# Local attention on one core: how the probabilities are transposed and the side values summed

## The chip, the cores and the metric

The kernel runs on one core of one Trainium2 chip. The metric is the device time of one execution in microseconds (us), the median of several runs.

The core has TensorE (PE in the rows; its weight loads are PEld), VectorE (DVE), ScalarE (ACT), GpSimd (POOL) and the sync engine (SP), each with an instruction queue of its own, worked off in order. They are tied together by semaphores: an instruction adds one when it is done, and another engine's queue stands at a wait until the count is there.

## The reference

Input x is 8 x 2048 x 512. A state-space convolution of it gives x2. On x2, two attentions are computed and added: a light one over all tokens, in windows, and a heavy one over 512 queries and 1024 keys that a routing picks. The change is in the light one:

```python
xn = layernorm(x); q, k, v = split(xn @ w_qkv, 3)        # 8 heads of 64
q, k, v -> windows of 64 tokens
kk, vv = around(k), around(v)      # each window sees the window before, itself, the window after: 192 keys
sim = (q * 64**-0.5) @ kk.T        # a missing neighbour (ends of the sequence) is masked
o = softmax(sim) @ vv
light = o @ w_out
```

All of it is fp32 in value: the big products are made of three fp32r products of high and low parts, the attention's own matmuls and transposes are fp32.

## The kernel before

The phases follow each other: preparation, convolution, light attention (from 570 to 2855 us of the profile), routing lists, heavy attention. Only `light_phase` is touched.

**The pipeline.** The light phase handles tiles of 128 tokens, 128 tiles in all (16 for each of 8 sequences). It is written as a software pipeline with one step per tile, numbered g (j is g modulo 16). Each engine has a function `body(g, j, live, b)` that issues its part of step g. `live(k)` says whether tile g-k exists. In step g, TensorE does, in this order:

1. `first_unit`: one quarter of a projection (q, k or v for 4 tiles at once), 12 matmuls of 512 columns, into PSUM bank `ps_b`
2. the output projection of tile g-10, into `ps_c`
3. a second unit into `ps_a`
4. `scores` of tile g-7 into `ps_s` (for each head and each of two windows, 192 key columns; `key_runs` splits them where the ring of keys or the order of columns breaks them)
5. `attend` of tile g-9 into `ps_d`: transposed probabilities times values, 8 matmuls for the tile's own 128 keys ("main", `pt_main`) and 8 for the two neighbouring half tiles ("side", `pt_side`, values in `val_side`)
6. `turn_side` and `turn_main` of tile g-8: transposes of the probabilities, side into `ps_c`, main of the even heads into `ps_b`, of the odd heads into `ps_a`
7. a third unit into `ps_d`
8. the transpose of the next tile's normalised x into `ps_c`

The four banks are shared: each is written in a step two or three times, and TensorE waits until an engine has copied it away (semaphores `..._kept`). Which unit is which goes round in four steps (`units(j)`): with r = (j + 1) mod 4 the first, second and third unit are

- r = 1: k2, k3, v0
- r = 2: v1, v2, v3
- r = 3: q0, q1, q2
- r = 0: q3, k0, k1 (of the next group)

**Who empties the banks.** VectorE copies the first unit out of `ps_b` (`u1_kept`) and the third out of `ps_d`, ScalarE the second out of `ps_a` (`u2_kept`). Two of these copies have a special place because they overwrite data that the scores of this step still read. In VectorE's body:

```python
first_query = units(j)[0][:2] == ("q", 0)
if live(4) and not first_query: wait(v, u1_made, g - 3); keep_unit(ps_b, units(j)[0], u1_kept)
...
if live(7):                      # waits s_made, then two reductions, neg_max (L1617)
...
if live(4) and first_query:      wait(v, u1_made, g - 3); keep_unit(ps_b, units(j)[0], u1_kept)
```

and in ScalarE's: `if live(7) and (j + 1) % GT in (0, 3): wait(act, s_made, g - 6)` ahead of `keep_unit(ps_a, units(j)[1], u2_kept)`.

**The softmax chain.** VectorE takes the maximum of the scores, ScalarE the exponentials (`exps`, into `prob`), VectorE the reciprocals, GpSimd multiplies `prob` by them (L1684, `p_normed`); TensorE transposes the result in the next step. After `attend`, ScalarE copies `ps_d` to `at_hi` (L1262), VectorE subtracts to `at_lo` (L1624, `o_kept`), and only then may the third unit write `ps_d`: `wait(pe, o_kept, g - 8); unit(ps_d, units(j)[2], u3_made)`.

SyncE issues the loads and stores in order, among them two DMAs per step that bring the neighbours' half tiles of `val` into `val_side`, a step before `attend` uses them.

## Time and profile before

| | us |
|---|---|
| median of 3 runs | 4286.02 (4284.94 to 4286.93) |
| the profiled execution's own time | 4281.34 |
| its span, first to last instruction | 4279.6 |
| light attention in it | about 570 to 2855 |
| PE busy, share of the span | 93% |
| DVE, ACT, POOL busy, share of the span | 66%, 42%, 20% |

A row of the timeline gives the start in us, the time from the first start to the last end in us, the engine, the line, the operation, output <- inputs, the tiling of the matmul array (rows*columns), the shape and the count (x). Ends of matmuls lie behind their starts by the pipeline's depth, so the cost of a group of matmuls is read from the start of one group to the start of the next. [n <-X] at the end means: the engine was idle for n us before it, and X released it.

### The profile page before, as it was taken

The numbers are of one execution on the slowest core, as the hardware profiler recorded it, in microseconds if no ns is written. First come the engines' busy times: TensorE is split into PE (matmuls) and PEld (weight loads), VectorE is DVE, ScalarE is ACT, GpSimd is POOL, SyncE is SP. The second block draws the span as 40 slices with busy tenths as digits, with TensorE's granted clock in tenths as the row PEclk, the third lists the DMA queues.
The fourth block names the chain that finished last, engine by engine and source line by source line (L and its number), as shares of the span: only waits on it lengthen the run. The fifth ranks groups of instructions, "written<-read, shape, count | busy, mean of one in ns | idle before, by whom it ended". The sixth has DMA issues, their size and how long they took to land. (4 is left out here: it accounts for less than half of the span.)

```text
span 4279.6 us, 96921 instructions
## 1 busy us (share of the span) xinstructions
PE 3973.7 (93%) x39328; PEld 3279.4 (77%) x39328; DVE 2820.8 (66%) x5012; ACT 1786.0 (42%) x4746; POOL 877.2 (20%) x663
## 2 busy tenths in 40 slices
PE   6788869999999999989999999968999999999998
PEld 5677757888888888878888888857677677677776
DVE  9888857776766767665555566674755646646546
ACT  7434324344433434434444433222544534534434
POOL 0222202222222222222222222211111011111011
PEclk9899979999999999999999999988999999999999
DMA  9688752222223222211222111122012022022021
GB/s 318 168 231 233 208 173 74 83 93 85 82 85 95 83 83 88 86 50 61 67 64 61 60 60 60 45 87 60 19 43 58 9 55 51 16 53 51 16 45 14
DMA packets 341371, 360.91 MB, mean 84 GB/s; under 512 B 23104, under 2 KB 237376, under 8 KB 340928
## 3 DMA queue, kind: packets, MB, share of 16 engines
q1 hardware_dynamic: 262592, 287.52, 22.5%
q0 software_dynamic: 12288, 33.56, 3.7%
q10 hardware_dynamic: 66048, 33.56, 2.9%
q8 instruction: 322, 5.28, 0.5%
q14 instruction: 121, 0.99, 0.1%
HBM read 228.21 MB, written 76.02 MB: 71 GB/s over the span
## 5 line engine op out<-in xcount | busy, mean ns | idle before, releaser
L1684 POOL TENSOR_TENSOR l_prob<-l_prob,l_inv 128x768 f32<-128x768 f32 x256 | 389.6, 1543 | 1690.9 <-DVE l_inv L1641 1690.9
L1235 ACT ACTIVATE l_prob<-l_ps_s,l_neg_max 128x192 f32<-128x192 f32 x1024 | 420.7, 443 | 7.5 <-DVE l_neg_max L1617 7.3
L2237 ACT ACTIVATE h_prob<-h_ps_s,h_neg_max 128x1024 f32<-128x1024 f32 x256 | 285.6, 1116 | 253.4 <-DVE h_neg_max L2311 253.4
L1617 DVE TENSOR_REDUCE l_neg_max<-l_ps_s 128x4 f32<-128x768 f32 x256 | 233.1, 952 | 238.5 <-PE l_ps_s L1004 219.4
L2308 DVE TENSOR_REDUCE h_neg_max<-h_ps_s 128x1 f32<-128x1024 f32 x256 | 312.3, 1220 | 99.7 <-PE h_ps_s L2100 91.0
L2365 DVE COPY h_probs_t<-h_ps_t 128x512 f32<-128x512 f32 x256 | 176.4, 689 | 143.1 <-PE h_ps_t L2112 142.9
L2127 PEld LDWEIGHTS h_ps_o<-h_probs_t,ahead_then_values 128*64 128x64 f32 x4096 | 221.6, 137 | 44.1 <-issue 43.0
L2127 PE MATMUL h_ps_o<-h_probs_t,ahead_then_values 128*64 128x128 f32 x4096 | 252.5, 276 | 0.0
L2112 PEld LDWEIGHTS h_ps_t<-ident,h_prob 64*128 64x128 f32 x4096 | 152.2, 140 | 121.7 <-ACT h_prob L2237 61.0
L1235 ACT ACTIVATION_READ_ACCUMULATOR l_prob<-l_ps_s,l_neg_max 128x1 f32 x1024 | 235.8, 230 | 0.0
L1004 PEld LDWEIGHTS l_ps_s<-l_k_t,l_q_t 64*64 64x64 f32 x6144 | 189.1, 133 | 48.1 <-issue 44.8
L2112 PE MATMUL h_ps_t<-ident,h_prob 64*128 64x64 f32 x4096 | 183.7, 230 | 44.7 <-ACT h_probs_t L2266 42.4
L1202 ACT ACTIVATE l_k_t<-l_ps_a,w_bias_k 128x512 f32<-128x512 f32 x64 | 44.0, 688 | 427.1 <-PE l_ps_a L721 184.4
L1004 PE MATMUL l_ps_s<-l_k_t,l_q_t 64*64 64x64 f32 (+2 forms) x6144 | 213.8, 277 | 2.9 <-DVE ahead_then_values L1498 2.9
L1363 DVE CUSTOM_DVE_ANT_0 l_dot_out<-ahead_then_values 128x512 f32<-128x512 f32 x240 | 205.8, 857 | 4.2
L719 PE MATMUL l_ps_c<-w_out_hi,l_at_hi 128*128 128x512 f32 x512 | 203.1, 397 | 5.8 <-DVE l_pt_side L1589 4.3
L2026 POOL TENSOR_TENSOR h_att<-w_null_v,h_null_exp 128x512 f32<-128x512 f32 x32 | 33.1, 1036 | 852.0 <-ACT h_null_exp L2274 852.0
L1608 DVE TENSOR_TENSOR l_res<-l_ps_c,l_xres 128x512 f32<-128x512 f32 x128 | 88.2, 689 | 176.9 <-PE l_ps_c L721 176.8
L720 PE MATMUL l_ps_c<-w_out_lo,l_at_hi 128*128 128x512 f32 x512 | 202.5, 395 | 0.0
L721 PE MATMUL l_ps_c<-w_out_hi,l_at_lo 128*128 128x512 f32 x512 | 201.6, 394 | 0.0
L1262 ACT ACTIVATE l_at_hi<-l_ps_d 128x512 fp32r<-128x512 f32 x128 | 76.4, 597 | 268.8 <-PE l_ps_d L1036 268.8
L1678 POOL TENSOR_TENSOR l_xres<-l_xres,w_row 128x512 f32<-128x512 f32 x128 | 179.1, 1399 | 16.9 <-DVE scores_then_results L1363 11.9
(392 smaller groups left out, 10793.2 us busy)
## 6 DMA issues: line engine op xcount, KB each, us to landing
toep_back<-taps_padded ACTq DMA_DIRECT2D x32, 1024.0 KB, 10.3
x<-xg SPq DMA_DIRECT2D x64, 512.0 KB, 8.7
l_xin<-x SPq DMA_DIRECT2D x128, 256.0 KB, 3.3
l_xres<-x SPq DMA_DIRECT2D x128, 256.0 KB, 3.2
l_val_side<-l_val SPq DMA_DIRECT2D x256, 128.0 KB, 3.1
out_dram<-l_res SPq DMA_DIRECT2D x128, 256.0 KB, 2.0
ahead_then_values<-x SPq DMA_DIRECT2D x126, 256.0 KB, 3.1
xin<-in_L_attn_x_dram SPq DMA_DIRECT2D x32, 768.0 KB, 6.3
```

The costliest lines, as they stand in the source:

```text
L719: nc.tensor.matmul(out, lh, rh, start=first, stop=False)
L720: nc.tensor.matmul(out, lh, rl, start=False, stop=False)
L721: return nc.tensor.matmul(out, ll, rh, start=False, stop=last)
L1004: last = nc.tensor.matmul(ps_s[win * WIN:(win + 1) * WIN, h, pair, col:col + n], q_t[rows, pair, t % GT * P + win * WIN:t % GT * P + (win ...
L1235: last = nc.scalar.activation(prob[t % 2][:, h, pair, :], ps_s[:, h, pair, BOTH], ACT.Exp, bias=neg_max[:, t % 2, h, pair:pair + 1], accum ...
L1363: nc.vector.tensor_tensor_reduce(dot_out[:, :], x_tile, w["rt"][:, r], 1.0, 0.0, ALU.mult, ALU.add, to[r]).then_inc(dot_step, 1)
L1617: nc.vector.tensor_reduce(neg_max[:, t % 2, h, :], ps_s[:, h, :, BOTH], AX_X, ALU.max, negate=True).then_inc(max_made, 1)
L1684: nc.gpsimd.tensor_tensor(mine, mine, spread(inv[:, t % 2, h, :], [1, PAIRS], [0, WIN + P]), ALU.mult).then_inc(p_normed, 1)
L2112: last = nc.tensor.transpose(ps_t[half][:, n, :], prob[i % 2][rows, n * P:(n + 1) * P], ident[rows, rows])
L2127: last = nc.tensor.matmul(ps_o[odd * DH:(odd + 1) * DH, k * P:(k + 1) * P], val[:, n, h * DH:(h + 1) * DH], probs_t[(2 * pair + odd) % 4][ ...
L2237: nc.scalar.activation(prob[i % 2][:, :].rearrange("p (a k) -> p a k", a=2), ps_s[i % 2][:, :, :], ACT.Exp, bias=neg_max[:, qt % 2, h:h + ...
L2308: nc.vector.tensor_reduce(at, ps_s[i % 2][:, :, :].rearrange("p a k -> p (a k)"), AX_X, ALU.max, negate=True).then_inc(max_step, 1)
```

## The change

- Transposes of main probabilities (`turn_main`): 16 of half the rows each (64 queries x 128 keys, with the 64 x 64 corner of the identity), alternately into `ps_b` (first window) and `ps_a` (second window); before, 8 of 128 x 128.
- Transposes of side probabilities (`turn_side`): `prob` is laid out so that the side columns of the two heads of a pair lie next to each other, and 4 transposes of 128 x 128 do what 16 matmuls with half an identity did. The columns of the even and odd head are laid out differently (`MAIN`, `SIDE`), and `key_runs` follows.
- Sums over side values (`attend_side`): 16 matmuls of 64 keys x 64 outputs x 64 queries, each on the rows that its head uses; before, 8 with 128 keys and 128 queries, half of them zeros. `pt_side` has half the size; the zeroing of `pt_side` and `val_side` goes away.
- `val_side` is laid out by window and head, filled by four DMAs of half the size instead of two; the value projection's weights are read in the order that puts the even heads first.
- VectorE copies the side probabilities with one copy of 128 partitions instead of two of 64, after the copy of `ps_b` instead of ahead of it.
- In TensorE's body the waits on `p_normed`, `u1_kept` and `u2_kept` are put together in `turns_ready`, which stands ahead of `attend_main`; the main transposes come ahead of the side ones.

```diff
@@ TensorE
-                def turn_main(bank, j, h, made):
+                def turns_ready(g):
+                    wait(pe, p_normed, 2 * (g - 7))
+                    wait(pe, u1_kept, done(g - 3))
+                    wait(pe, u2_kept, done(g - 2))
+
+                def turn_main(j):
+
+                    for n in range(HEADS):
+                        pair, h = n // 2, n % 2
+                        for rows, bank, made in ((LO, ps_b, main0_made), (HI, ps_a, main1_made)):
+                            last = nc.tensor.transpose(bank[:, n * WIN:(n + 1) * WIN],
+                                                       prob[j % 2][rows, pair, h, MAIN[h]], ident[rows, rows])
+                            if n == HEADS - 1:
+                                last.then_inc(made, 1)
+
+                def turn_side(j):
+
                     for pair in range(PAIRS):
-                        last = nc.tensor.transpose(bank[:, pair * P:(pair + 1) * P], prob[j % 2][:, h, pair, MAIN],
+                        last = nc.tensor.transpose(ps_c[:, pair * P:(pair + 1) * P],
+                                                   prob[j % 2][:, pair, :, :].rearrange("p h c -> p (h c)")[:, SIDES],
                                                    ident[:, :])
-                    last.then_inc(made, 1)
-
-                def turn_side(j):
-
-
-                    for n in range(HEADS):
-                        side, cols = prob[j % 2][:, n // PAIRS, n % PAIRS, SIDE], slice(n * WIN, (n + 1) * WIN)
-                        if j != NCH - 1:
-                            last = nc.tensor.matmul(ps_c[LO, cols], side, ident[:, HI], start=True, stop=True)
-                        if j != 0:
-                            last = nc.tensor.matmul(ps_c[HI, cols], side, ident[:, LO], start=True, stop=True)
                     last.then_inc(side_made, 1)
 
-                def attend(j):
-
-
-                    for keys, probs in ((val[:, j % RING], pt_main), (val_side[:, j % 2], pt_side)):
-                        for n in range(HEADS):
-                            h, pair = n % 2, n // 2
-                            last = nc.tensor.matmul(ps_d[h * DH:(h + 1) * DH, pair * P:(pair + 1) * P],
-                                                    keys[:, n * DH:(n + 1) * DH], probs[:, h, pair, :],
-                                                    start=(probs is pt_main and pair == 0),
-                                                    stop=(probs is pt_side and pair == PAIRS - 1), skip_group_check=True)
+                def attend_main(j):
+                    for pair in range(PAIRS):
+                        for h, rows in enumerate((LO, HI)):
+                            mine = h * HDH // 2 + pair * DH
+                            nc.tensor.matmul(ps_d[rows, pair * P:(pair + 1) * P], val[:, j % RING, mine:mine + DH],
+                                             pt_main[:, pair, h, :], start=(pair == 0), stop=False, skip_group_check=True)
+
+                def attend_side(j):
+                    for pair in range(PAIRS):
+                        for win, queries in enumerate((LO, HI)):
+                            for h, rows in enumerate((LO, HI)):
+                                at = pair * P + win * WIN
+                                last = nc.tensor.matmul(ps_d[rows, at:at + WIN],
+                                                        val_side[rows, j % 2, win, pair * DH:(pair + 1) * DH],
+                                                        pt_side[rows, pair, queries], start=False,
+                                                        stop=(pair == PAIRS - 1 and win == 1), skip_group_check=True)
                     last.then_inc(o_made, 1)
...
                         if tasks:
                             sum_taken(*tasks[0])
-                        attend(t)
+                        if live(8):
+                            turns_ready(g)
+                        attend_main(t)
+                        attend_side(t)
+                    elif live(8):
+                        turns_ready(g)
                     if live(8):
-                        t = (j - 8) % NCH
-                        wait(pe, p_normed, 2 * (g - 7))
+                        turn_main((j - 8) % NCH)
                         wait(pe, res_made, g - 9)
-                        turn_side(t)
-                        wait(pe, u1_kept, done(g - 3))
-                        turn_main(ps_b, t, 0, main0_made)
-                        wait(pe, u2_kept, done(g - 2))
-                        turn_main(ps_a, t, 1, main1_made)
+                        turn_side((j - 8) % NCH)
@@ scores
+        MAIN, SIDE = (slice(0, P), slice(WIN, WIN + P)), (slice(P, P + WIN), slice(0, WIN))
+        BOTH, SIDES = slice(0, WIN + P), slice(P, 2 * P)
+
+        def key_runs(j, win, h):
 
             at, end = j % RING * P, RING * P
...
+            side = (at + P if win else at - WIN) % end
+            if (j, win) in ((0, 0), (NCH - 1, 1)):
+                return [(MAIN[h].start, at, P)]
+            if h and side + WIN == at or not h and at + P == side:
+                return [(0, min(at, side), WIN + P)]
+            return [(MAIN[h].start, at, P), (SIDE[h].start, side, WIN)]
@@ SyncE
-                        for keys, tile in ((LO, at if at == NCH - 1 else at + 1), (HI, at if at == 0 else at - 1)):
-                            sp.dma_start(val_side[keys, j % 2, :], val[keys, tile % RING, :]).then_inc(side_in[j % 2], 16)
+                        for win, keys, tile in ((0, HI, at if at == 0 else at - 1), (1, LO, at if at == NCH - 1 else at + 1)):
+                            for h, rows in enumerate((LO, HI)):
+                                sp.dma_start(val_side[rows, j % 2, win, :],
+                                             val[keys, tile % RING, h * HDH // 2:(h + 1) * HDH // 2]).then_inc(side_in[j % 2], 16)
@@ value projection
-                            right = w["qkv_hi"][:, k, 2 * HDH:QKV], w["qkv_lo"][:, k, 2 * HDH:QKV]
+                            right = (w[part][:, k, 2 * HDH:QKV].rearrange("p (a h d) -> p h a d", h=2, d=DH)
+                                     for part in ("qkv_hi", "qkv_lo"))
@@ VectorE
                     if live(8):
+                        wait(v, main0_made, g - 7)
+                        nc.vector.tensor_copy(pt_main[:, :, :, LO],
+                                              ps_b[:, :].rearrange("p (a h q) -> p a h q", h=2, q=WIN)).then_inc(main0_kept, 1)
                         wait(v, side_made, g - 7)
-                        keep_side((j - 8) % NCH)
-                        wait(v, main0_made, g - 7)
-                        nc.vector.tensor_copy(pt_main[:, 0, :, :].rearrange("p a q -> p (a q)"),
-                                              ps_b[:, :]).then_inc(main0_kept, 1)
+                        nc.vector.tensor_copy(pt_side[:, :, :].rearrange("p a q -> p (a q)"), ps_c[:, :]).then_inc(side_kept, 1)
```

ScalarE's copy of `ps_a` goes to `pt_main[:, :, :, HI]`; `exps` and GpSimd's scaling only change the order in which they address `prob`.

## Rows read from the trace of the kernel before

**Rows 1.** Busy time in stretches, light phase: window, length, busy us of each engine (instructions), granted clock.

```profile
700.00:1100.00 400.00, 396.10 (x4060) 335.88 (x4061) 285.72 (x578) 161.71 (x502) 106.23 (x70) 1.00 0.28 87
```

**Rows 2.** Timeline, TensorE, step g = 41 from its scores to its third unit.

```profile
1215.38 1.66 PE L1004 MATMUL l_ps_s<-l_k_t,l_q_t 64*64 64x192 f32 x48
1216.97 1.09 PE L1036 MATMUL l_ps_d<-l_pt_main,l_val 128*64 128x128 f32 x16
1217.89 1.04 PE L1036 MATMUL l_ps_d<-l_pt_side,l_val_side 128*64 128x128 f32 x16
1218.76 0.22 PE L1025 MATMUL l_ps_c<-ident,l_prob 128*64 128x64 f32 x1
...
1219.80 0.66 PE L1015 MATMUL l_ps_b<-ident,l_prob 128*128 128x128 f32 x4
1220.29 0.60 PE L1015 MATMUL l_ps_a<-ident,l_prob 128*128 128x128 f32 x4
1220.64 0.48 PE L719 MATMUL l_ps_d<-w_qkv_hi,l_xt_hi 128*128 128x512 f32 x1
```

**Rows 3.** Timeline, the same step: ScalarE and VectorE behind attend, and the DMAs.

```profile
1216.97 1.11 SPq L944 DMA_DIRECT2D l_val_side<-l_val  x2
...
1218.98 0.60 ACT L1262 ACTIVATE l_at_hi<-l_ps_d 128x512 fp32r<-128x512 f32 x1 [2.64 <-PE l_ps_d L1036]
...
1219.61 0.69 DVE L1624 TENSOR_TENSOR l_at_lo<-l_ps_d,l_at_hi 128x512 fp32r<-128x512 f32 x1
...
1220.22 1.38 DVE L1589 COPY l_pt_side<-l_ps_c 64x512 f32<-64x512 f32 x2
```

**Rows 4.** Timeline, first (g = 10) and last (g = 130) of 31 steps with r = 3.

```profile
685.61 1.09 PE L1036 MATMUL l_ps_d<-l_pt_main,l_val 128*64 128x128 f32 x16
685.72 1.82 DVE L1617 TENSOR_REDUCE l_neg_max<-l_ps_s 128x4 f32<-128x768 f32 x2 [1.68 <-PE l_ps_s L1004]
...
687.46 0.74 DVE L1300 TENSOR_SCALAR l_q_t<-l_ps_b,w_bias_q 128x512 f32<-128x512 f32 x1
...
693.27 3.34 POOL L1684 TENSOR_TENSOR l_prob<-l_prob,l_inv 128x768 f32<-128x768 f32 x2 [11.20 <-DVE l_inv L1641]
...
2769.77 1.09 PE L1036 MATMUL l_ps_d<-l_pt_main,l_val 128*64 128x128 f32 x16
...
2771.62 0.74 DVE L1300 TENSOR_SCALAR l_q_t<-l_ps_b,w_bias_q 128x512 f32<-128x512 f32 x1
```

**Rows 5.** Timeline, the first and last of 30 steps with r = 0 (g = 11, g = 127).

```profile
704.29 1.09 PE L1036 MATMUL l_ps_d<-l_pt_main,l_val 128*64 128x128 f32 x16
704.46 0.69 ACT L1202 ACTIVATE l_k_t<-l_ps_a,w_bias_k 128x512 f32<-128x512 f32 x1 [10.40 <-PE l_ps_s L1004]
...
2718.47 1.09 PE L1036 MATMUL l_ps_d<-l_pt_main,l_val 128*64 128x128 f32 x16
2718.63 0.69 ACT L1202 ACTIVATE l_k_t<-l_ps_a,w_bias_k 128x512 f32<-128x512 f32 x1 [10.48 <-PE l_ps_s L1004]
```

**Rows 6.** Timeline: VectorE's at_lo releases TensorE in step g = 13.

```profile
742.23 0.68 DVE L1624 TENSOR_TENSOR l_at_lo<-l_ps_d,l_at_hi 128x512 fp32r<-128x512 f32 x1
...
742.97 0.50 PE L719 MATMUL l_ps_d<-w_qkv_hi,l_xt_hi 128*128 128x512 f32 x1 [0.91 <-DVE l_at_lo L1624]
```

**Rows 7.** Timeline, TensorE in the heavy phase: transposes of 64 rows into two banks.

```profile
3501.63 0.71 PE L2112 MATMUL h_ps_t<-ident,h_prob 64*128 64x64 f32 x16 [2.09 <-ACT h_probs_t L2266]
3502.13 0.51 PE L2100 MATMUL h_ps_s<-h_k_hi,h_q_hi 64*128 64x512 f32 x2
```

**Rows 8.** Timeline, TensorE, step g = 40, whose side transposes have only one half.

```profile
1201.85 1.09 PE L1025 MATMUL l_ps_c<-ident,l_prob 128*64 128x64 f32 x16
1202.88 0.66 PE L1015 MATMUL l_ps_b<-ident,l_prob 128*128 128x128 f32 x4
```

**Rows 9.** Timeline and busy time in stretches: a long wait of TensorE in step g = 9, and the clock around it.

```profile
672.34 0.50 PE L719 MATMUL l_ps_d<-w_qkv_hi,l_xt_hi 128*128 128x512 f32 x1 [2.77 <-DVE l_at_lo L1624]
...
665.00:672.00 7.00, 4.46 (x86) 3.80 (x77) 6.69 (x18) 4.31 (x11) 0.75 (x1) 1.00 0.47 149
```

More of the change, by code:

```diff
@@ L776, in light_phase @@
         val = sb("l_val", [P, RING, HDH])
-        val_side = sb("l_val_side", [P, 2, HDH])
-        prob = [sb(f"l_prob{i}", [P, 2, PAIRS, WIN + P]) for i in range(2)]
+        val_side = sb("l_val_side", [P, 2, 2, HDH // 2])
+        prob = [sb(f"l_prob{i}", [P, PAIRS, 2, WIN + P]) for i in range(2)]
         neg_max = sb("l_neg_max", [P, 2, 2, PAIRS])
@@ L783, in light_phase @@
         wall = sb("l_wall", [P, 1])
-        pt_main = sb("l_pt_main", [P, 2, PAIRS, P])
-        pt_side = sb("l_pt_side", [P, 2, PAIRS, P])
+        pt_main = sb("l_pt_main", [P, PAIRS, 2, P])
+        pt_side = sb("l_pt_side", [P, PAIRS, P])
         at_hi = sb("l_at_hi", [P, KC, P], F32R)
@@ L818, in light_phase @@
              "out_made res_made").split())
[L819 removed]
+        ZEROED = 2
         ident = keep["ident"]
         LO, HI = slice(0, WIN), slice(WIN, P)
[L823 to L825 removed]
+        MAIN, SIDE = (slice(0, P), slice(WIN, WIN + P)), (slice(P, P + WIN), slice(0, WIN))
+        BOTH, SIDES = slice(0, WIN + P), slice(P, 2 * P)
+        def key_runs(j, win, h):
             at, end = j % RING * P, RING * P
[L828 to L836 removed]
+            side = (at + P if win else at - WIN) % end
[4 more added lines that the diff above has]
+            return [(MAIN[h].start, at, P), (SIDE[h].start, side, WIN)]
         def units(j):
@@ L1002, in scores @@
                             rows = slice(h * DH, (h + 1) * DH)
-                            for col, key, n in key_runs(t, win):
+                            for col, key, n in key_runs(t, win, h):
                                 last = nc.tensor.matmul(
@@ L1008, in scores @@
                             if (t, win) in ((0, 0), (NCH - 1, 1)):
-                                last = nc.tensor.matmul(ps_s[win * WIN:(win + 1) * WIN, h, pair, SIDE], ident[rows, rows],
+                                last = nc.tensor.matmul(ps_s[win * WIN:(win + 1) * WIN, h, pair, SIDE[h]], ident[rows, rows],
                                                         spread(wall[rows, :], [0, WIN]), start=True, stop=True)
                     last.then_inc(s_made, 1)
-                def turn_main(bank, j, h, made):
+                def turns_ready(g):
+                    wait(pe, p_normed, 2 * (g - 7))
+                    wait(pe, u1_kept, done(g - 3))
+                    wait(pe, u2_kept, done(g - 2))
@@ L1140, in body @@
                         wait(pe, u3_kept, done(g - 3))
-                        wait(pe, side_in[(j - 9) % 2], (g - j) * 16 + 32 * ((j - 9) // 2 + 1))
+                        wait(pe, side_in[(j - 9) % 2], (g - j) * 32 + 64 * ((j - 9) // 2 + 1))
                         if tasks:
                             sum_taken(*tasks[0])
-                        attend(t)
+                        if live(8):
[4 more added lines that the diff above has]
+                        turns_ready(g)
                     if live(8):
-                        t = (j - 8) % NCH
-                        wait(pe, p_normed, 2 * (g - 7))
+                        turn_main((j - 8) % NCH)
                         wait(pe, res_made, g - 9)
-                        turn_side(t)
-                        wait(pe, u1_kept, done(g - 3))
-                        turn_main(ps_b, t, 0, main0_made)
-                        wait(pe, u2_kept, done(g - 2))
-                        turn_main(ps_a, t, 1, main1_made)
+                        turn_side((j - 8) % NCH)
                     if live(3):
@@ L1234, in exps @@
                     for pair in range(PAIRS):
-                        last = nc.scalar.activation(prob[t % 2][:, h, pair, :], ps_s[:, h, pair, BOTH], ACT.Exp,
+                        last = nc.scalar.activation(prob[t % 2][:, pair, h, :], ps_s[:, h, pair, BOTH], ACT.Exp,
                                                     bias=neg_max[:, t % 2, h, pair:pair + 1],
@@ L1267, in body @@
                         wait(act, main1_made, g - 7)
-                        nc.scalar.activation(pt_main[:, 1, :, :].rearrange("p a q -> p (a q)"), ps_a[:, :],
+                        nc.scalar.activation(pt_main[:, :, :, HI], ps_a[:, :].rearrange("p (a h q) -> p a h q", h=2, q=WIN),
                                              ACT.Identity).then_inc(main1_kept, 1)
@@ L1581, in _ @@
                 keep_xt_lo(0, 0)
-                def keep_side(j):
-                    for rows, at, cut in ((LO, slice(WIN, P), j == NCH - 1), (HI, slice(0, WIN), j == 0)):
-                        to = pt_side[rows, :, :, at]
-                        if cut:
-                            last = nc.vector.memset(to, 0.0)
-                        else:
-                            last = nc.vector.tensor_copy(to, ps_c[rows, :].rearrange("p (h a q) -> p h a q", h=2, q=WIN))
-                    last.then_inc(side_kept, 1)
                 def body(g, j, live, b, routing=False):
@@ L1682, in body @@
                         for h in range(2):
[L1683 removed]
+                            mine = prob[t % 2][:, :, h, :]
                             nc.gpsimd.tensor_tensor(mine, mine, spread(inv[:, t % 2, h, :], [1, PAIRS], [0, WIN + P]),
```

15 lines of the change are left out of this document (removed).

## The prediction

> **What bounds the kernel now.** Three views, in this order. First the busy time by stretches, to see which engine the light phase hangs on: in 400 us of it TensorE is busy for 396.1 us at full clock (1.00, the 2.4 GHz level), VectorE for 286, ScalarE for 162 [rows 1]. TensorE runs without a gap, so whatever shortens its queue pays, if nobody makes it wait instead, and every wait that the change adds is paid in full. Second, TensorE's timeline over one step, to see what each part costs from start to start. Step 41 [rows 2], counted from S, the start of attend (1216.97): main sums 0.92 us, side sums 0.87, side transposes 1.04, main transposes 0.49 and 0.35, third unit at S + 3.67. The next step's attend starts at 1233.89, so a step is 16.92 us. Third, the timelines of VectorE and ScalarE beside it, to see when each bank is free again. Two things are to be seen there. ScalarE's at_hi starts 0.22 us after the side transposes have started and at_lo ends at 1219.61 + 0.69 = 1220.30 [rows 3], 1.54 us after attend has left TensorE (1218.76). The third unit needs that at_lo and starts at 1220.64: a margin of 0.34 us. And two of the bank copies come late: in the steps with r = 3 VectorE copies q0 out of `ps_b` only after the two maxima, and is done at 687.46 + 0.74 = S + 2.59 [rows 4]; with r = 0 ScalarE copies k0 out of `ps_a` after the scores, and is done at 704.46 + 0.69 = S + 0.86 [rows 5]. Today TensorE asks for the first only when it begins the main transposes (S + 2.83), for the second at S + 3.32, so it waits for neither.
>
> **The new place of the waits.** `turns_ready` asks for `u1_kept` and `u2_kept` of this very step ahead of `attend_main`, so attend, the transposes and all behind them stand still until the copies are done. Nothing can fill the gap, for TensorE's queue is in order and everything that it could do is behind the wait. The copies don't come earlier: VectorE's maxima start when the scores are done (0.11 us after S) and ScalarE's copy waits for the same scores. From the end of a releasing instruction to the start of the matmul that it frees it took 742.97 - (742.23 + 0.68) = 0.06 us in step 13 [rows 6].
> - r = 3, whose copy ended at S + 2.59 in the first and the last of 31 steps (g = 10, 14, ... 130): 2.65 us each, 31 x 2.65 = 82.2 us. Here `u2_kept` (q1) ends earlier, so it adds nothing.
> - r = 0, 30 steps (g = 11 ... 127): the copy ends at S + 0.86 or S + 0.85 at first and last (some in between are 0.06 earlier); I take 0.84 + 0.06 = 0.90 us, 30 x 0.90 = 27.0 us.
> - r = 1 and 2: the copies are over before S. Nothing.
> - `p_normed`, also moved ahead: GpSimd is done at 693.27 + 3.34 = 696.6, and the next attend starts at 704.29 [rows 4, 5]. 7.7 us to spare; a stall shifts both alike. Nothing.
>
> Sum of added waits: 109.2 us.
>
> **TensorE's own work.** Main sums: same 16 instructions (an fp32 matmul is two in the trace), 0.92 us. Side sums: 16 matmuls, so 32 instructions of 64 columns, on two diagonal corners of the array, 16 each. No row of before has this form. Nearest: when the side transposes of step 40 use one half of the array's columns only, 16 instructions of 64 columns in one corner take 1202.88 - 1201.85 = 1.03 us [rows 8], the change of form included; and the two corners go side by side (32 of them took 1.04 in step 41). That makes 0.93 to 1.03 us, if two row halves run side by side as two column halves did. The transposes of half the rows in the heavy phase show row halves doing that: 16 in 0.50 us [rows 7], less than the 16 x 0.065 of one corner. Lower bound: the scores push 6144 columns (4 pairs x 4 x 192, twice) through in 1.59 us; at that density these 2048 take 0.53 us. Upper bound: one after another at 0.065 us, 2.1 us. I take 0.93, plus 0.10 for a change of the array's form between main and side sums: the first of two like groups of transposes costs 0.49 and the second 0.35 [rows 2], so a change costs about 0.1. Attend ends at S' + 1.95 in place of S + 1.80, where S' is its delayed start.
>
> The transposes become 0.50 (the heavy phase's form is exactly this one) + 0.35 + about 0.1 twice = 1.05 us in place of 1.88. But the third unit can't follow at once. at_lo is ready 1.54 us after attend's end and releases 0.06 later, at S' + 3.55, while TensorE is done with its transposes at S' + 3.0. So of 0.83 us of transposes saved, 3.67 - 3.55 = 0.12 us per step remain, the rest turns into a wait on `o_kept`. Over the 122 steps with such a unit and an attend (g = 9 to 130, of which three or four are held by other things): -15 us.
>
> The Trainium skill says that changing the tiling mode drains TensorE (TensorEngine Tiling (Array Packing), Tiling Modes, Key Properties). The trace agrees with the 0.49 against 0.35 above. Without such a drain my step would be 0.1 us shorter and the sum 12 us less.
>
> **The rest.** Scores: the same number of matmuls and columns, in other runs: 48 instructions in six of eight tiles and the doubled runs of a wrapped ring moved from one tile to another. The first two of each pair now have equal runs (128 + 64 each) and the last two 192 each, where before a 192 ran beside a 128 + 64. I take 0; bounds: two row halves perfectly side by side are 8 x 384 columns / 2.4 GHz = 1.28 us against 1.59, -0.3 us; 0.15 the other way: -37 to +18 us. VectorE's side copy is halved (two took 1.38 us [rows 3]), but VectorE has 28% idle and nothing waits for it there: main then side copy end at about S' + 4.9, the x transpose that needs `ps_c` comes at S' + 6.4; if this cover were gone, it would still be 0.7 us earlier than the 1.38 + 0.69 of now. The four half-size DMAs: SyncE's two issues take 1.11 us [rows 3], four 2.2; behind them only the x load for two steps later and the look-ahead load wait, and the data are used a step (17 us) later. Nothing. The value unit's operand read in another order, and the strided writes of copies: the same counts, 0. The removed zeroings lie where VectorE then waits for loads, 0. The drain after the last tile: five steps held by VectorE's routing work, where one copy less and shorter transposes should give about 2 us, -2.
>
> Sum: 109.2 - 15 - 2 = +92 us. Against the profiled execution, 4281.3 + 92 = 4373 (span 4372). The runs' median is 4.7 us above it: 4286.0 + 92 = 4378 us, 2.1% slower.
>
> **The rivals.**
> - *Side sums don't run side by side* (0.10). Both row halves now write one bank, `ps_d`; everywhere in the trace where two row halves alternate (scores, heavy transposes), they write different banks. If the hardware keeps them apart, 32 instructions cost up to 2.1 us instead of 0.93: +1.15 us x 122 = +140, 4518 us. It decides from 1.3 us on for that group, where it adds 45 us. The Trainium skill states that different row tiles can't access the same PSUM bank at once (TensorEngine Tiling (Array Packing), Gotcha 1: PSUM Pressure); no row of before has the case.
> - *Side sums as dense as can be* (0.13). At 0.53 us attend ends 0.40 us earlier, and since at_lo follows attend, all of it reaches the third unit: -49 us, 4329 us. Speaks for it: the scores use all four corners, too, with as short runs among them. Against: the 58 to 65 ns of one corner.
> - *The waits are met earlier than I read* (0.04), the only way to be faster: were `u1_kept` there at S, as with r = 1 and 2, the added waits would fall to nothing and only -17 would stay: 4269 us, 0.4% faster. It decides from a wait of 0.28 us, where 61 waits equal the gains (61 x 0.28 = 17). Against it: the maxima are on the same queue ahead of the copy, in all 31 steps.
> - *The scores get faster by the even runs* (0.03): with all four corners busy they'd take 6144 / 4 columns = 0.64 us, -0.95 x 122 = -116, 4262 us. Nothing in the rows shows such a density.
> - *The clock falls in the new waits* (0.05): A stretch at half speed as long as the wait costs half of it, 1.3 us, 31 times: +41, 4419 us. Against: after a wait of 2.77 us in step 9 the granted clock stayed 1.00 [rows 9].
>
> **How the numbers follow.** My forecast has 0.65, its own range (scores, side sums 0.85 to 1.05) 4350 to 4400. The range with no more than 2 in 10 outside takes in the dense side sums and the clock: 4325 to 4425; the bank rival lies above it. Within 0.2% is about what a measurement of this kernel can't tell from no change. Faster by more: the third and fourth rival, 0.06; within: 0.02; slower: 0.92.
>
> **What would show it.** After the change: TensorE idle 2.6 us ahead of the main sums released by VectorE's `l_q_t`, 31 times, and 0.9 us released by ScalarE's `l_k_t`, 30 times; 0.4 to 0.7 us idle ahead of the third unit in every step, released by `l_at_lo`; steps of r = 1 and 2 at 16.8 us, of r = 3 at 19.4, of r = 0 at 17.7; the side sums' group 0.9 to 1.05 us long; TensorE's busy share in the light phase down from 99% to about 93%. Wrong would be: the copies ready at S, or side sums of 0.5 or 2 us.

## The result: 3.4% slower, beyond the forecast's range

The changed kernel takes 4435.0 us (median of 4 runs, 4432.3 to 4438.5), the kernel before 4285.5 in the same comparison: ratio 1.0336, 95% interval 1.0320 to 1.0352, that is +149.5 us. The forecast had the direction and most of the mechanism, but +92 us, 4378 (4325 to 4425). The profiled execution took 4434.3 us with a span of 4432.3, 152.7 more than the span of before.

Busy time by stretches of the changed kernel's light phase, the answer to [rows 1] (columns: stretch, length, busy us of PE, PEld, DVE, ACT, POOL with instructions, granted clock, DMA share, GB/s):

```profile
700.00:1100.00 400.00, 370.25 (x3687) 302.80 (x3688) 251.19 (x510) 151.04 (x476) 101.44 (x66) 0.98 0.26 78
```

TensorE went from 99% busy to 92.6%, and its clock is not quite full any more. Who makes it wait, from the view of waits (engine, tile, line, releaser, us in total, times, longest):

```profile
PE l_ps_d L1041 <- DVE l_q_t L1311: 86.2, 31, 2.9
...
PE l_ps_d L1041 <- ACT l_k_t L1215: 28.0, 30, 0.9
...
PE l_ps_d L719 <- DVE l_at_lo L1626: 21.7, 109, 0.5
```

The three waits of the forecast are there with its releasers, the first two also with its numbers of times. The third was forecast in all 122 steps at 0.4 to 0.7 us; it is there in 109, and mostly 0.20 us long. An undisturbed step, g = 41, answers to [rows 2]; TensorE's timeline:

```profile
1264.44 1.66 PE L1005 MATMUL l_ps_s<-l_k_t,l_q_t 64*64 64x128 f32 x48
1266.03 1.09 PE L1041 MATMUL l_ps_d<-l_pt_main,l_val 128*64 128x128 f32 x16
1267.05 1.15 PE L1049 MATMUL l_ps_d<-l_pt_side,l_val_side 64*64 64x64 f32 x32
1268.13 0.27 PE L1024 MATMUL l_ps_b<-ident,l_prob 64*128 64x64 f32 x1
...
1268.77 0.66 PE L1032 MATMUL l_ps_c<-ident,l_prob 128*128 128x128 f32 x4
1269.62 0.50 PE L719 MATMUL l_ps_d<-w_qkv_hi,l_xt_hi 128*128 128x512 f32 x1 [0.20 <-DVE l_at_lo L1626]
```

From start to start: scores 1.59 as before, main sums 1.02, side sums 1.08, main transposes 0.64, side transposes 0.85 with 0.20 idle at their end until at_lo comes, third unit at S' + 3.59 (3.67 before). Two r = 3 steps, TensorE and the releasing copy:

```profile
1212.04 0.74 DVE L1311 TENSOR_SCALAR l_q_t<-l_ps_b,w_bias_q 128x512 f32<-128x512 f32 x1
...
1213.03 1.98 PE L1041 MATMUL l_ps_d<-l_pt_main,l_val 128*64 128x128 f32 x16 [2.77 <-DVE l_q_t L1311]
1214.94 1.64 PE L1049 MATMUL l_ps_d<-l_pt_side,l_val_side 64*64 64x64 f32 x32
...
1285.74 1.09 PE L1041 MATMUL l_ps_d<-l_pt_main,l_val 128*64 128x128 f32 x16 [2.78 <-DVE l_q_t L1311]
1286.76 1.15 PE L1049 MATMUL l_ps_d<-l_pt_side,l_val_side 64*64 64x64 f32 x32
```

Both waited alike. Behind the first wait the main sums took 1.91 us and the side sums 1.57, behind the second 1.02 and 1.08. Busy time in stretches of the first (g = 38) shows why; the column to read is the one behind POOL's, the granted clock:

```profile
1208.00:1210.00 2.00, 2.00 (x59) 1.64 (x57) 0.65 (x2) 0.00 (x0) 0.00 (x0) 1.00 0.88 234
1210.00:1213.00 3.00, 0.26 (x10) 0.07 (x2) 2.48 (x3) 0.69 (x1) 0.00 (x0) 0.94 0.72 215
1213.00:1214.00 1.00, 0.97 (x10) 1.00 (x12) 0.00 (x0) 0.00 (x0) 0.00 (x0) 0.50 0.17 64
1214.00:1215.00 1.00, 1.00 (x12) 0.67 (x8) 0.00 (x0) 0.00 (x0) 0.00 (x0) 0.50 0.07 16
1215.00:1216.00 1.00, 1.00 (x21) 1.00 (x22) 0.00 (x0) 0.00 (x0) 0.00 (x0) 0.50 0.00 0
1216.00:1217.00 1.00, 1.00 (x34) 0.93 (x30) 0.00 (x0) 0.37 (x1) 0.00 (x0) 0.97 0.00 0
```

Three us at 0.50, the 1.2 GHz level, right behind the idle time, and 1.00, 2.4 GHz, ahead of it. Read step by step, the third unit came at S' + 3.60 in 11 of the 31 r = 3 steps, and 0.94 to 2.02 us later in the other 20, 26.2 us in all. Step 9, which has r = 2, shows the same behind a wait of 3.88 us: side sums 1.90 us, third unit at S' + 4.86.

### The profile page after: what moved, and what is told of

It reads as the page before. It is cut to its first block and busy times, and to the rows that moved or that the text cites. A ratio compares the mean times of both kernels' runs of the same rounds, so it can differ in the third digit from the quotient of the medians.

```text
span 4432.3 us, 96608 instructions
## 1 busy us (share of the span) xinstructions
PE 3979.8 (90%) x39072; PEld 3220.7 (73%) x39072; DVE 2724.6 (61%) x4882; ACT 1784.1 (40%) x4746; POOL 878.3 (20%) x663
## 5 line engine op out<-in xcount | busy, mean ns | idle before, releaser
L1041 PE MATMUL l_ps_d<-l_pt_main,l_val 128*64 128x128 f32 x2048 | 152.0, 293 | 119.6 <-DVE l_q_t L1311 86.2
L1626 DVE TENSOR_TENSOR l_at_lo<-l_ps_d,l_at_hi 128x512 fp32r<-128x512 f32 x128 | 88.5, 691 | 226.0 <-ACT l_at_hi L1275 223.7
L1041 PEld LDWEIGHTS l_ps_d<-l_pt_main,l_val 128*64 128x64 f32 x2048 | 120.2, 145 | 137.5 <-issue 130.1
```

The costliest lines, as they stand in the source:

```text
L1041: nc.tensor.matmul(ps_d[rows, pair * P:(pair + 1) * P], val[:, j % RING, mine:mine + DH], pt_main[:, pair, h, :], start=(pair == 0), stop= ...
```

## The experiments

All times below are medians; the kernel before, run beside them, had 4285.8 to 4288.3. "Steps 9 to 130" is the time in the trace from the start of the sums in step 9 to that in step 131, which leaves out the stages that no edit touches: 2125.0 us before, 2260.0 in the changed kernel.

**The waits alone, in the kernel before**

```diff
+                        if live(8):
+                            turns_ready(g)
                         attend(t)
...
-                        wait(pe, p_normed, 2 * (g - 7))
                         wait(pe, res_made, g - 9)
                         turn_side(t)
-                        wait(pe, u1_kept, done(g - 3))
                         turn_main(ps_b, t, 0, main0_made)
-                        wait(pe, u2_kept, done(g - 2))
                         turn_main(ps_a, t, 1, main1_made)
```

> The kernel before with only the three waits of the transposes moved ahead of the sums, everything else as it was. Forecast's terms (latency 0.06 us, no change of clock): 31 x 2.65 + 30 x 0.90 = +109, about 4395 us. Terms as read from the changed kernel: 31 x 2.85 + 30 x 1.01 = +119, and +26 where the granted clock falls behind the long waits: about 4430 us, with main and side sums 1 to 2 us longer in some two thirds of the r = 3 steps. Rival: the slow sums come from the new 64 x 64 form and not from the wait: +119 alone, 4405 us, all sums at their old 0.92 and 0.87 us.

Measured: 4437.4 us, ratio 1.0341 (1.0320 to 1.0361). Steps 9 to 130 took 2266.7 us, +141.7. View of waits, and TensorE's timeline in steps g = 38 and 42:

```profile
PE l_ps_d L1041 <- DVE l_q_t L1306: 86.1, 31, 2.9
...
PE l_ps_d L1041 <- ACT l_k_t L1208: 27.5, 30, 0.9
```

```profile
1214.05 1.09 PE L1041 MATMUL l_ps_d<-l_pt_main,l_val 128*64 128x128 f32 x16 [2.77 <-DVE l_q_t L1306]
1214.95 1.07 PE L1041 MATMUL l_ps_d<-l_pt_side,l_val_side 128*64 128x128 f32 x16
...
1285.65 1.97 PE L1041 MATMUL l_ps_d<-l_pt_main,l_val 128*64 128x128 f32 x16 [2.77 <-DVE l_q_t L1306]
1287.39 1.53 PE L1041 MATMUL l_ps_d<-l_pt_side,l_val_side 128*64 128x128 f32 x16
```

The three moved waits alone, with every old matmul, make the whole loss. The slow sums come with them too, in the old form: main sums 0.90 us behind one wait, 1.74 behind the next. In 18 of 31 steps the third unit was late, 27.4 us in all. The forecast's own terms (4395) and the rival without the clock (4405) fall.

**The waits put back in the changed kernel**

```diff
@@ turns_ready
                     wait(pe, p_normed, 2 * (g - 7))
-                    wait(pe, u1_kept, done(g - 3))
-                    wait(pe, u2_kept, done(g - 2))
@@ turn_side
                     for pair in range(PAIRS):
+                        if pair == PAIRS - 1:
+                            wait(pe, u1_kept, done(g - 3))
+                            wait(pe, u2_kept, done(g - 2))
@@ body
-                        if live(8):
-                            turns_ready(g)
                         attend_main(t)
                         attend_side(t)
...
-                        turn_main((j - 8) % NCH)
+                        turns_ready(g)
                         wait(pe, res_made, g - 9)
-                        turn_side((j - 8) % NCH)
+                        turn_side((j - 8) % NCH, g)
+                        turn_main((j - 8) % NCH)
```

> The changed kernel with the waits on the two bank copies taken from ahead of the sums and put behind three of the four side transposes, which now stand ahead of the main ones. Theory (the loss is the waits, and a slower clock behind the long ones): no idle time ahead of the sums, none behind either, because the first three side transposes end at about S + 2.4 us, the last copy of the r = 3 steps at S + 2.59, and all transposes are over by S + 3.5, when the third unit waits for at_lo anyway (S + 3.60 in the changed kernel, S + 3.67 before). So 122 x -0.07 = -9 us against the kernel before: about 4277 us. Rival 1: the convolution and weight stages, which start the light phase 9.9 us later in the profile of the changed kernel, are part of the change: about 4286. Rival 2: the new sums and transposes themselves cost more than their timelines show, and the waits are only where it is booked: above 4320.

Measured: 4285.5 us, ratio 1.0004 (0.9994 to 1.0013). The whole loss is gone, and the new sums and transposes bring nothing that shows in the time. TensorE's timeline in step g = 38, with r = 3:

```profile
1172.43 1.09 PE L1042 MATMUL l_ps_d<-l_pt_main,l_val 128*64 128x128 f32 x16
1173.45 1.15 PE L1050 MATMUL l_ps_d<-l_pt_side,l_val_side 64*64 64x64 f32 x32
1174.53 0.87 PE L1033 MATMUL l_ps_c<-ident,l_prob 128*128 128x128 f32 x4
...
1176.02 0.50 PE L719 MATMUL l_ps_d<-l_xt_hi,w_qkv_hi 128*128 128x512 f32 x1
```

The late copy costs a little inside the side transposes (0.87 in place of 0.66) and nothing at the end: the third unit starts at S + 3.59. Ordinary steps are 16.86 to 16.90 us against 16.92, and all steps 9 to 130 together are 2.7 us less. Single steps came out longer (g = 9: 21.70 against 20.29, g = 63: 20.70 against 18.73) or shorter (g = 79: 31.27 against 32.56). In the two longer ones the granted clock fell to 0.50, behind idle times of 2.39 and 2.01 us that no edit made. So of the expected 9 us less, 2.7 are in the steps and none in the time.

**One of the two waits put back**

```diff
@@ turns_ready
                     wait(pe, p_normed, 2 * (g - 7))
-                    wait(pe, u1_kept, done(g - 3))
                     wait(pe, u2_kept, done(g - 2))
@@ turn_side
                     for pair in range(PAIRS):
+                        if pair == PAIRS - 1:
+                            wait(pe, u1_kept, done(g - 3))
```

The side transposes stand ahead of the main ones here as well.

> The changed kernel with only the wait on the first unit's copy moved back (behind three side transposes, which stand ahead of the main ones); the wait on the second unit's copy stays ahead of the sums. Theory: the second unit's copy follows the scores on ScalarE with r = 3 as with r = 0, so 61 waits of 1.0 us stand ahead of the sums, and none of 2.8; waits of 1.0 us cost no clock: 4277 + 61 = about 4338 us. Rival (the clock falls behind any wait ahead of the sums, by about half of its length): 4338 + 30 = 4368 us. If the second unit's copy were late by itself as much as the first one's: 4435.

Measured: 4363.5 us, ratio 1.0178 (1.0161 to 1.0195), between the two numbers expected. View of waits:

```profile
PE l_ps_d L1042 <- ACT l_q_t L1216: 28.6, 31, 0.9
PE l_ps_d L1042 <- ACT l_k_t L1216: 28.0, 30, 0.9
...
PE l_ps_b L719 <- issue: 15.6, 4, 4.9
```

The 61 waits are 0.9 us long, and no step had slow sums behind one: the third unit is at S' + 3.59 to 3.61 in all 31 r = 3 steps. So a clock that falls behind these waits, too, is refuted, though the time alone, 5 us from the rival's 4368 and 25 from the theory's 4338, would have spoken for it. Of these 25 us, 8.5 are the base (4285.5 with both waits back, not 4277), and 3.7 are one more wait in step 9, for ScalarE's value copy. 13.2 are in three single steps at the end of the loop over 16 tiles (g = 31, 47, 63: 5.1, 4.4 and 3.7 us longer than with both waits back), where TensorE stands idle for "issue" for 4.4 to 4.9 us; behind each of these three the granted clock fell to 0.50. Why this program is idle there for so long and the others for 1.2 to 2.1 us wasn't tried.

**The long wait filled with work**

```diff
                         if live(8):
+                            if live(3) and (j + 1) % GT == 3:
+                                for _ in range(10):
+                                    nc.tensor.matmul(ps_d[:, :], w["qkv_hi"][:, 0, 0:P], w["qkv_hi"][:, 1, 0:512],
+                                                     start=True, stop=True)
                             turns_ready(g)
```

> The changed kernel with ten matmuls of 512 columns in the r = 3 steps ahead of the waits, into the bank that the sums then start anew: about 2.1 us of work inside a wait of 2.85 us, so that the wait ends when it did but TensorE is idle for only some 0.6 us. Clock theory: the sums behind it run at full clock in all 31 steps, 26 us less than the changed kernel: about 4409 us. Rival: the sums behind the wait are slow for a reason other than idle time (contention with VectorE's or ScalarE's copies, a weight load): 4435 us as before the filling.

> The changed kernel with five matmuls of 512 columns in the long wait in place of ten: TensorE idle for some 1.6 us in place of 2.8 (none), 0.6 (ten). Theory (the granted clock falls only behind an idle time of about the full 2.8 us; behind 1.0 us it never did): the sums run at full clock in all r = 3 steps, 4394 us as with ten. Rival (the clock falls behind any idle time over a microsecond, as part of the cases did behind 2.8): 4400 to 4410, with some slow r = 3 steps.

Measured: 4394.0 us with ten (ratio 1.0248, 1.0231 to 1.0265), 4397.9 with five (1.0260, 1.0242 to 1.0278), against 4435 of the changed kernel, though 310 or 155 useless matmuls were added. Timeline of step g = 38, with ten and then with five:

```profile
1197.66 2.56 PE L1160 MATMUL l_ps_d<-w_qkv_hi 128*128 128x512 f32 x10
...
1200.35 1.09 PE L1041 MATMUL l_ps_d<-l_pt_main,l_val 128*64 128x128 f32 x16
```

```profile
1202.70 1.43 PE L1160 MATMUL l_ps_d<-w_qkv_hi 128*128 128x512 f32 x5
1205.39 1.09 PE L1041 MATMUL l_ps_d<-l_pt_main,l_val 128*64 128x128 f32 x16 [1.26 <-issue]
1206.42 1.15 PE L1049 MATMUL l_ps_d<-l_pt_side,l_val_side 64*64 64x64 f32 x32
```

In both, not one of the 31 r = 3 steps has slow sums. The ten took 2.56 us instead of the 2.1 expected, so TensorE was idle for 0.10 to 0.13 us there and not for 0.6; with five it was idle for 1.26 to 1.28. Steps 9 to 130 took 2231.5 and 2232.0 us, 28 less than in the changed kernel, about the 26.2 us of the clock (the sums also start 0.10 us behind the copy's end in step 38 in place of 0.25, which would be 4.6 more). Five do as well as ten. The other 13 and 9 us of the way from 4435 lie outside the steps, in stages that vary by themselves (see the kernel before, unchanged); what they are due to isn't shown.

**The order of the waits, for their price**

```diff
                     wait(pe, p_normed, 2 * (g - 7))
-                    wait(pe, u1_kept, done(g - 3))
                     wait(pe, u2_kept, done(g - 2))
+                    wait(pe, u1_kept, done(g - 3))
```

> The changed kernel with the two waits on the bank copies in the other order: the second unit's copy first, the first unit's last. In the changed kernel TensorE started 0.26 us after the end of the late copy with r = 3 (where one more wait stood behind it) and 0.15 us after it with r = 0 (where it was the last wait), against the 0.06 us of a single wait that the forecast took. Theory (each wait that stands behind the late one costs another 0.1 us): 0.15 us and stalls of 2.68 with r = 3, 0.25 us and stalls of 1.03 with r = 0; the time is that of the changed kernel, 4435 us. Rival (the latency belongs to the releasing engine): 0.26 and 0.15 stay as they are.

Measured: 4435.4 us in one run. Timeline, step g = 38 (r = 3) and the sums of step 39 (r = 0):

```profile
1207.25 0.74 DVE L1311 TENSOR_SCALAR l_q_t<-l_ps_b,w_bias_q 128x512 f32<-128x512 f32 x1
...
1208.14 1.09 PE L1041 MATMUL l_ps_d<-l_pt_main,l_val 128*64 128x128 f32 x16 [2.67 <-DVE l_q_t L1311]
...
1225.20 0.69 ACT L1215 ACTIVATE l_k_t<-l_ps_a,w_bias_k 128x512 f32<-128x512 f32 x1 [8.67 <-PE l_ps_s L1010]
...
1226.14 1.10 PE L1041 MATMUL l_ps_d<-l_pt_main,l_val 128*64 128x128 f32 x16 [1.05 <-ACT l_k_t L1215]
```

From the copy's end to the sums' start: 1208.14 - 1207.99 = 0.15 with r = 3 (0.25 in the changed kernel: 1213.03 - 1212.78), and 1226.14 - 1225.89 = 0.25 with r = 0 (0.14 there). The 0.1 us went with the wait that stands behind the late one, whatever engine releases it. It isn't a fixed price of that wait: with the useless matmuls ahead, the same order of waits took 0.10 us in all 31 r = 3 steps.

**The side sums through one corner after the other**

```diff
-                    for pair in range(PAIRS):
-                        for win, queries in enumerate((LO, HI)):
-                            for h, rows in enumerate((LO, HI)):
+                    for h, rows in enumerate((LO, HI)):
+                        for pair in range(PAIRS):
+                            for win, queries in enumerate((LO, HI)):
```

> As the kernel with the waits behind three side transposes (4285.5 us), but the 16 side sums go first all through one corner of the array and then all through the other, not by turns. The changed kernel's 32 side-sum instructions took 1.08 us until the next group started. Theory (two corners run side by side although both write one bank; one corner alone takes some 0.06 us for each instruction): 32 x 0.06 = 1.9 to 2.0 us, the third unit 0.9 us later in each of 122 steps: 4285 + 110 = about 4395 us. Rival (instructions of 64 columns are this fast in any order, so the forecast's overlap is no overlap): 1.1 us and 4285 us.

Measured: 4378.1 us, ratio 1.0220 (1.0200 to 1.0240), against 4285.5 with the turns. Timeline, step 41:

```profile
1244.59 1.09 PE L1042 MATMUL l_ps_d<-l_pt_main,l_val 128*64 128x128 f32 x16
1245.61 1.90 PE L1050 MATMUL l_ps_d<-l_pt_side,l_val_side 64*64 64x64 f32 x32
1247.44 0.66 PE L1033 MATMUL l_ps_c<-ident,l_prob 128*128 128x128 f32 x4
...
1248.92 0.50 PE L719 MATMUL l_ps_d<-w_qkv_hi,l_xt_hi 128*128 128x512 f32 x1 [0.19 <-DVE l_at_lo L1624]
```

1.83 us in place of 1.08, and all of the 0.75 reaches the third unit (S + 4.33), since at_lo hangs on the end of the sums. 122 x 0.74 = 90 us; measured 92.6. By turns, then, the two corners do run side by side, and into one bank. The rival "side sums don't run side by side" is refuted. What the prediction quoted from the Trainium skill (TensorEngine Tiling (Array Packing), Gotcha 1: PSUM Pressure) doesn't hold for this pattern, two row halves that write different partitions of `ps_d`: 1.08 us against 1.83 for the same instructions one corner after the other.

**The kernel before, unchanged**

> The kernel before, unchanged, for a second profile: the light phase began at 569.5 us in the first profile of it and at 575 to 579 us in those of all other kernels, though nothing ahead of it differs. Theory (variation from run to run of the convolution's stage): the start of the light phase lies between 569 and 580 us, not bound to 569.5. Rival (each other program's layout costs these 5 to 9 us): 569.5 again.

Measured: 4295.4 us in one run. The last copy of the weights' stage, ahead of the light phase, on VectorE's timeline, in the first profile of the kernel before, and then in this one:

```profile
559.71 0.43 DVE L671 COPY lw_wide<-lw_bias_v 128x512 f32<-128x512 f32 x1
```

```profile
569.50 0.43 DVE L671 COPY lw_wide<-lw_bias_v 128x512 f32<-128x512 f32 x1
```

The same program is 9.8 us later here; the changed kernel's row is at 568.86. Steps 9 to 130 took 2125.9 us, against 2125.0. So the stages ahead vary by some 10 us from execution to execution, and the steps are good to 1 us: what the edits do has to be read there.

This second profile also holds the wait of step 9 on which the prediction's reading of the clock rests [rows 9]. Busy time in the 2 us behind that wait, in the first profile; then TensorE's timeline and the same stretch in this one:

```profile
672.34:674.34 2.00, 2.00 (x9) 1.65 (x10) 1.96 (x4) 2.00 (x10) 0.00 (x0) 1.00 0.00 0
```

```profile
680.39 0.79 PE L719 MATMUL l_ps_d<-w_qkv_hi,l_xt_hi 128*128 128x512 f32 x1 [2.77 <-DVE l_at_lo L1624]
```

```profile
680.39:682.39 2.00, 2.00 (x5) 1.61 (x6) 1.96 (x4) 2.00 (x10) 0.00 (x0) 0.50 0.00 0
```

The same program, the same wait of 2.77 us, and the clock was 1.00 behind it once and 0.50 the other time.

**A version that is faster than both**

With the waits back, TensorE is idle for 0.2 us in the steps with r = 0, 1 and 2 until at_lo comes, between its transposes and the third unit. In the steps with r = 1 and 2 the sums can go ahead of the scores (base: the kernel with the waits back):

```diff
+                    sums_first = live(3) and live(9) and (j + 1) % GT in (1, 2)
-                    if live(7):
+                    if live(7) and not sums_first:
                         scores(j)
...
                         attend_side(t)
+                    if live(7) and sums_first:
+                        scores(j)
@@ VectorE, ahead of the two maxima
+                    if sums_first:
+                        keep_at_lo()
```

> As the kernel with the waits behind three side transposes (4285.5 us), and in the steps with r = 1 and 2 the sums stand ahead of the scores on TensorE, and VectorE makes at_lo ahead of the two maxima. In a step the third unit starts 3.60 us after the sums for at_lo alone, 0.5 us after the transposes; with 1.59 us of scores between sums and transposes at_lo is there first, and the third unit starts 2.10 + 1.59 + 1.15 = 4.8 us after the sums' start against 1.59 + 3.60 = 5.2 after the scores' start. Theory (the chain behind the sums swallows the saved transposes): 60 x 0.4 = 24 us less, about 4262 us, 0.5% faster than either kernel. Rival (the maxima, 2.1 us later, now come last for the bank copies, the x transpose or the next step's sums): the gain shows as idle time elsewhere, 4285 us or more.

> The same, but only in steps without routing work (up to step 79): 35 x 0.4 = 14 us less, about 4271 us. Rival (the sums, 1.6 us earlier in the steps with routing work, meet VectorE's unfinished bit or log step there): this kernel is the faster of the two, because the other one loses in those steps.

Measured: 4258.4 us in all such steps, ratio 0.9933 (0.9921 to 0.9946), and 4265.4 up to step 79, 0.9948 (0.9935 to 0.9960). The first is 29 us faster than the kernel before (4287.8 beside it) and 27 faster than the one with the waits back (4285.5, in another comparison), and the steps with routing work add their part, so the rivals of both runs fall. Steps 9 to 130 took 28.6 and 20.3 us less than with the waits back; about 3 of each are what that kernel had lost to the clock in steps 9 and 63. TensorE in step 41, and VectorE's at_lo:

```profile
1210.46 1.09 PE L1042 MATMUL l_ps_d<-l_pt_main,l_val 128*64 128x128 f32 x16
1211.49 1.15 PE L1050 MATMUL l_ps_d<-l_pt_side,l_val_side 64*64 64x64 f32 x32
1212.47 1.61 PE L1005 MATMUL l_ps_s<-l_k_t,l_q_t 64*64 64x128 f32 x48
1214.01 0.66 PE L1033 MATMUL l_ps_c<-ident,l_prob 128*128 128x128 f32 x4
1215.23 0.50 PE L719 MATMUL l_ps_d<-w_qkv_hi,l_xt_hi 128*128 128x512 f32 x1
```

```profile
1213.31 0.69 DVE L1620 TENSOR_TENSOR l_at_lo<-l_ps_d,l_at_hi 128x512 fp32r<-128x512 f32 x1 [0.18 <-ACT l_at_hi L1276]
```

at_lo is ready at 1214.00, 1.2 us ahead of the third unit, which starts 4.77 us after the first of sums and scores instead of 1.59 + 3.60 = 5.19. 61 x 0.42 = 26 us. Not all of it is at_lo's chain: from the first transpose to the third unit it is 1.22 us against 1.50, 0.28 less. Sums and scores together are shorter by the other 0.14 (3.55 against 1.59 + 2.10), now that the side sums and the scores behind them have one array form, 64*64.

The same edit of order in the kernel before:

> The kernel before with the sums ahead of the scores in the steps with r = 1 and 2, the edit that took 27 us off the changed kernel with its waits put back. In the kernel before the transposes (1.88 us) last longer than the chain from the sums to at_lo (1.54 us), so there is nothing for the scores to cover. Theory: no gain, within 5 us of 4286. Rival (the other order is worth it by itself, with any form of the transposes): 4260 us, as with the new form.

Measured: 4296.6 us, ratio 1.0019 (1.0007 to 1.0031), 8 us slower than the kernel before beside it, a little more than the 5 us expected at most. The third unit starts 5.41 us after the first of sums and scores, against 1.59 + 3.68 = 5.27, and steps 9 to 130 took 6.3 us more. With the old transposes nothing waits for at_lo in an ordinary step, so there is nothing to cover. The rival, the other order being worth 27 us with any form, is refuted.

## Why the prediction fell short

**Right.** The two late copies and their 61 waits, by number, place and releaser. The change of array form between main and side sums (sums 1.02 in place of 0.92). The side sums at 1.08 (taken: 0.93; its upper bound was 1.03 without the form change behind it), neither dense nor one after another, so both rivals on them are out. Scores unchanged at 1.59. That the saved transposes hardly reach the end, because at_lo comes last. There two errors nearly cancel, and that is luck: the sums took 2.10 us and not 1.95, at_lo was ready 1.44 us behind them and not 1.54 (in step 41 it ended at 1268.88 + 0.69 = 1269.57). The transposes took 1.3 us and not 1.05, so the idle time ahead of the third unit is 0.20 us and not 0.4 to 0.7.

**The step that failed: the clock.** The prediction set "the clock falls in the new waits" apart as a rival with 0.05, and so took 0 for it in the sum. It leaned on one wait of 2.77 us in step 9 [rows 9]. The stretch shown there ends at 672.00, ahead of the end of the wait at 672.34, so it doesn't show the clock behind it. That clock was 1.00 in this profile, but 0.50 behind the same wait in the second profile of the same kernel. The trace of before had more to read. Of eight waits of 2.08 or 2.09 us in its heavy phase the clock fell to 0.50 behind three. Here is one in the timeline and in busy time; [rows 7] begins with one behind which it stayed at 1.00:

```profile
3333.36 0.55 PE L2112 MATMUL h_ps_t<-ident,h_prob 64*128 64x64 f32 x6 [2.09 <-ACT h_probs_t L2266]
```

```profile
3333.36:3335.36 2.00, 2.00 (x22) 1.81 (x24) 0.74 (x2) 1.69 (x3) 0.00 (x0) 0.52 0.04 8
```

Behind the change's 31 long waits it fell in 20 (18 with the old sums), and took 26 us; filling the wait gave them back, with five matmuls as well as with ten. The rival's own price, +41, was of the right size, for it counted all 31 times.

**Sizes that were off.** Against the span:

| term | forecast | measured |
|---|---|---|
| r = 3 waits | 31 x 2.65 = 82 | 31 x 2.85 = 88 |
| r = 0 waits | 30 x 0.90 = 27 | 30 x 1.01 = 30 |
| clock | 0 | +26 |
| third unit earlier | -15 | 122 x -0.08 = -10 |
| steps 9 to 130 | +94 | +135.0 |
| wait ahead of the sums of step 9 | 0 | +3.9 |
| all else | -2 | +13.8 |
| span | +92 | +152.7 |

The waits were taken too short by their latency: 0.06 us from one single wait [rows 6], where three stood in a row and it took 0.14 and 0.25. The wait of 3.9 us in step 9, and one of 0.84 us in step 13, both for ScalarE's value copy, were overlooked; the forecast had nothing for r = 2 and didn't look at the first steps. Of the last 13.8 us, 9.2 lie ahead of the weights' last copy (568.86 against 559.71), and there the kernel before moved by 9.8 on its own. So the first profile of before was an early one, and part of the 152.7 is probably no effect of the change. Between the medians' +149.5 and the +139 found in the steps and in step 9's wait 10.5 us remain, which these runs don't settle. In the two kernels with the filled wait nothing remains: their medians rise by 108 and 110 us, their steps with that wait by 110 and 111.

**Which part lost.** Only the place of the waits: alone they cost 152 us, and without them the rest of the change costs nothing and gains nothing in the time (1.0004). The rest became worth 27 us with the sums ahead of the scores in half of the steps, some two thirds of it because other work covered the chain to at_lo.

## What to carry to other kernels

In an in-order queue a wait belongs right ahead of the first instruction that needs it; grouping three of them ahead of 2 us of work that needs none cost 3.4%. Work taken off the bounding engine pays only if the next thing it needs is ready: look up the chain that starts at the end of the shortened part, and reorder so that other work covers it. And when a stall is priced, price the clock behind it as a term of the sum with its odds, read from all waits of like length in the trace, not as a rival that either holds or doesn't.

## What was not expected of the hardware

- Behind an idle time of 2.8 us TensorE's granted clock fell to its lower level in 20 of 31 equal cases, at 0.94 to 2.02 us each, and did not in 11. Behind 0.9 us (61 cases) and behind 1.3 us (31 cases, five matmuls ahead) it never fell. Behind 2.08 or 2.09 us it fell in three of eight cases in the kernel before, and behind 3.6 to 4.9 us in all nine of the light phase (step 9 of six kernels, the three loop ends above). What decides between equal cases stays open.
- A wait can cost time though it was fulfilled long ago: 0.14 us from release to start when the late one stands last of two or three, 0.25 when another stands behind it, but 0.10 in that order with useless matmuls ahead.
- 32 instructions of 64 columns, by turns in two diagonal corners and into one bank, took 1.08 us from start to start; one corner after the other 1.83, 0.057 each.
- The same program's idle time for "issue" at the loop's end was 1.2 to 2.1 us in all kernels but one, and up to 4.9 us in that one.
